# Third stage of a two-layer gated cross-attention model: the causal mask of the fifth unit written by VectorE and ScalarE

## The chip, the cores and the metric

The kernel runs on one core of a Trainium2 chip. The metric is the device time of one execution in microseconds; three executions of the kernel before gave 1333.63, 1334.13 and 1334.41.

## The reference

The model has two layers of gated cross-attention and a gated feed-forward part each, on x of 16 sequences of 128 tokens and 512 channels. The change touches the attention of the second layer only:

```
qp = q @ Wq.T;  k, v = split(latent_kv @ Wkv_expand.T)      # 16 heads of 32
scores = einsum('bhqd,bhkd->bhqk', qh, kh) / sqrt(32)
scores = where(causal, scores, finfo.min)                   # causal, 128 x 128
attn = softmax(scores);  out = (attn @ vh) @ Wout.T
x = x + tanh(g_xattn[1]) * out                              # q is layernorm(x)
```

## The kernel before, in words

The kernel is written by hand for the five engines, each with its own program (`tensor`, `vector`, `scalar`, `gpsimd`, `sync`), and semaphores between them. The order of the work on each engine is the order in which these programs issue it. There is no planner. Four stages follow each other: attention and feed-forward of the first layer, attention of the second (the third stage), feed-forward of the second.

The third stage goes over 16 units, numbered 0 to 15. Unit u stands for a group of four sequences (u // 4) and a group of four heads (u % 4). Its scores fill four banks of PSUM, banks 4 to 7, one for each head j; in a bank each sequence has a block of 128 columns. Per unit:

- TensorE (`scores3`, line 954) writes the mask into each bank: a product of the identity `idb` with the mask `mkb` (bf16, 0 or -1e30) that overwrites the bank. Then 16 products of queries and keys, four per bank, are added to it (`start` is False). Each of them shows as two in the trace.
- VectorE (`largest`, 1920) reads each bank and takes the negated row maxima.
- ScalarE (`exp3`, 1401) reads each bank in four pieces: the exponential with the maximum as bias, and the sum of each row.
- VectorE (`inverse`) inverts the sums, GpSimd multiplies, VectorE's block transposes and a trip through DRAM turn heads 0 and 1, TensorE (`turn3`) turns heads 2 and 3, and TensorE (`av3`) multiplies with the values. ScalarE and VectorE split that result into a rounded part and a remainder (the shape 128x512 into `AR`).

In some units the mask comes another way. `seeded(u)` (line 543) tells them. There `scores3` leaves out the four products, and `seed3(u, j)` copies `mkb` into the bank once the exponentials of unit u - 1 have read it; the banks j in `by_vector(u)` (line 550: bank 0 alone where u % 4 is 1, else 0 and 1) are written by VectorE (line 1915), the others by ScalarE (line 1413). In these units the bank counts as free for TensorE only when `seed3` is done; in the others it is free when the exponentials are. Before the change the units 7, 8, 9, 11, 12, 13 and 15 are seeded.

The programs walk through steps; in step u, TensorE issues: scores of unit u - 1, queries of u (12 products), keys of u (3), values' products of u - 3, the output projection if one is due (from step 7 on), transposes of u - 2, transposes of the next layer norm. VectorE issues in step u: the four maxima of unit u - 1, block transposes of u - 2, the copy of the queries of u, two inverses of u - 1, then `seed3(u, j)` if u is seeded, the copy of the keys of u, the remainder of the values' product, and small work on the layer norm. ScalarE: the exponentials of unit u - 1, the rounding of the values' product of u - 3, `seed3(u, j)` if u is seeded, the copies of the transposed probabilities. In the steps 3 to 7 (`k_first`, line 547) the rounding comes behind all 16 exponentials, and in later steps among them. The scores of unit u itself are issued at the head of step u + 1.

Of the kernel before, what the change touches and what calls it, by code (L numbers as in the profile page):

```python
# [180 lines left out]
def build(nc, i, out):  # L181
    ctx = ExitStack()
    with ctx:
# [357 lines left out]


        def seeded(u):
            return 7 <= u < 16 and u % 4 != 2


        def k_first(u):
# [10 lines left out]
        def exps_over(u, j):  # L558
            return ex_ok["3", u, j] if seeded(u + 1) else ps.drained(("s3", u, j))
# [8 lines left out]
        def tensor(pe):  # L568
# [385 lines left out]
            def scores3(u):  # L954

                ks = [ps.take(("s3", u, j), 4 + j) for j in range(4)]
                pe.wait_ge(*d_ib[1])
                for j in range(4):
                    pe.wait_ge(*ps.free(("s3", u, j)))
                    if not seeded(u):  # L960
                        pe.matmul(blocks3(ks[j]), idb[:, :], mask3, True, False)
                pe.wait_ge(*ps.drained(("q3", u)))
                pe.wait_ge(*ps.drained(("k3", u)))
                for b in range(4):
                    s = slice(128 * b, 128 * b + 128)
                    for j in range(4):
                        ins = pe.matmul(ks[j][:, s], Q3[32 * j:32 * j + 32, s], K3[32 * j:32 * j + 32, s], False, True)
                        if b == 3:
                            ins.then_inc(*ps.fill(("s3", u, j)))
# [166 lines left out]
        def scalar(ac):  # L1136
# [264 lines left out]
            def exp3(u, js):  # L1401
                for j in js:
                    S, k = sm3[:, u % 2, j, :], ps.ap(("s3", u, j))
                    ac.wait_ge(*nb_ok["3", u, j])
                    if u >= 2:
                        ac.wait_ge(*(p3y_ok[u - 2, j] if j < 2 else ps.full(("pt3", u - 2, j))))
                    for b in range(4):
                        c = 512 * j + 128 * b
                        ins = ac.act(P3[:, u % 2, c:c + 128], k[:, 128 * b:128 * b + 128], ACT.Exp, bias=S[:, b:b + 1],
                                     scale=1.0, accum_out=S[:, 4 + b:5 + b])  # L1410
                    ins.then_inc(*(ex_ok.mark(("3", u, j)) if seeded(u + 1) else ps.drain(("s3", u, j), on_act)))
# [1319 lines left out]
```

## Time and profile before

| | |
|---|---|
| median of three runs | 1334.13 us (1333.63 to 1334.41) |
| profiled execution | 1333.26 us |
| its span, first to last instruction | 1331.5 us |
| TensorE busy | 1310.9 us, 98% |
| VectorE busy | 938.0 us, 70% |
| ScalarE busy | 518.0 us, 39% |
| GpSimd busy | 404.9 us, 30% |
| granted TensorE clock, mean | 1.00 |

Times in the rows are microseconds from the start of the span. A line number is that of the helper that issues the operation: L118 a product, L121 a transpose on TensorE, L124 any activation of ScalarE, L127 a copy, L146 the maxima, L130 an operation on two tensors. Tensors that share memory go by one name: `MSK` holds the queries and keys of the third stage, `P` its probabilities, `sm` maxima and sums, `PTV` the turned probabilities. DVE is VectorE, ACT is ScalarE, PE is TensorE.

### The profile page before, as it was taken

To read this page: it belongs to the slowest core of one execution; us is meant where nothing else is said; L and a number is where in the kernel's file an instruction comes from. 1 tells how busy PE (TensorE), PEld (TensorE's weight loads), DVE (VectorE), ACT (ScalarE), POOL (GpSimd) and SP (SyncE) were. 2 spreads that over 40 slices of the span, in tenths; PEclk is the share of its full clock that TensorE was granted. 3 is DMA by queue.
4 is the path that set the end of the run, shared out by engine and by line. 5 is a ranking of instruction groups with operands and counts; after the bars stand their busy time and mean duration, and the time that the engine had idled before them with its cause. 6 is when DMAs were issued, how large, how long until landed. Compare 5 with 4: busy or idle time off the path is not lost.

```text
span 1331.5 us, 20246 instructions
## 1 busy us (share of the span) xinstructions
PE 1310.9 (98%) x7348; PEld 1063.1 (80%) x7348; DVE 938.0 (70%) x1813; ACT 518.0 (39%) x1569; POOL 404.9 (30%) x462
## 2 busy tenths in 40 slices
PE   7999999999999999999999999999998999999998
PEld 6888888888887788878887888788886777778887
DVE  5766676675775878785678668776888888846643
ACT  3545455454564322231113111321127788832220
POOL 4212323231255342201111111113435866630000
PEclk9999999999999999999999999999999999999999
DMA  8755454443572222210121112112334556465651
GB/s 302 236 169 164 148 170 140 154 158 122 187 218 88 86 86 79 80 44 17 52 83 35 50 40 88 44 49 62 93 96 144 191 191 207 159 206 174 215 165 56
DMA packets 135987, 167.92 MB, mean 126 GB/s; under 512 B 16080, under 2 KB 87888, under 8 KB 135888
## 3 DMA queue, kind: packets, MB, share of 16 engines
q1 hardware_dynamic: 135888, 166.63, 39.4%
q8 instruction: 58, 0.95, 0.3%
q14 instruction: 41, 0.34, 0.1%
HBM read 112.05 MB, written 54.53 MB: 125 GB/s over the span
## 4 chain that ended last, share of the span: by engine, by line
PE 89%; DVE 5%; ACT 3%; DMA 1%; issue 1%; POOL 0%; SPq 0%; DVEq 0%; ACTq 0%; POOLq 0%
PE bank L118 87%; ACT P L124 2%; PE bank L121 2%; DVE STG L130 1%; DVE AH L130 1%; DVE st L152 1%; DVE XR L140 1%; DVE sm L146 0%; ACT STG L124 0%; DVE AH L127 0%; ACT AR L124 0%; DMA XR<-in_x_dram 0%; DMA STG<-in_WqT_dram 0%; ACT bank L124 0%; DVE AR L130 0%
## 5 line engine op out<-in xcount | busy, mean ns | idle before, releaser
L118 PE MATMUL bank<-XT,AR 128*128 128x512 f32 x1152 | 279.7, 392 | 0.1
L118 PE MATMUL bank<-AR 128*128 128x512 f32 x1056 | 257.7, 395 | 0.5 <-DVE MSK L136 0.4
L118 PEld LDWEIGHTS bank<-XT,AR 128*128 128x128 f32 x1152 | 214.2, 188 | 47.0 <-ACT STG L124 0.5
L124 ACT ACTIVATE STG<-bank,b1c 128x512 f32<-128x512 f32 x128 | 88.4, 690 | 384.6 <-PE bank L118 309.5
L118 PEld LDWEIGHTS bank<-AR 128*128 128x128 f32 x1056 | 194.4, 188 | 48.5 <-issue 3.1
L118 PE MATMUL bank<-AR,CT 128*128 128x512 f32 x768 | 191.3, 392 | 0.0
L118 PE MATMUL bank<-AR,AH 128*128 128x512 f32 x768 | 185.5, 390 | 0.0
L127 DVE CAST AH<-STG 128x512 fp32r<-128x512 f32 x192 | 90.5, 471 | 110.7 <-PE bank L118 99.0
L118 PEld LDWEIGHTS bank<-AR,AH 128*128 128x128 f32 x768 | 143.9, 188 | 30.0 <-DVE AH L130 0.2
L118 PEld LDWEIGHTS bank<-AR,CT 128*128 128x128 f32 x768 | 140.2, 188 | 26.8
L127 POOL CAST BA<-STG 128x256 fp32r<-128x256 f32 x64 | 30.7, 479 | 393.5 <-PE bank L118 240.8
L130 DVE TENSOR_TENSOR AH<-STG,AH 128x512 fp32r<-128x512 f32 x192 | 141.5, 737 | 6.6
L124 ACT ACTIVATE Pb<-bank,sm 128x128 f32<-128x128 f32 x256 | 90.1, 377 | 89.5 <-DVE sm L136 89.4
L130 POOL TENSOR_TENSOR Pb<-Pb,sm 128x512 f32<-128x512 f32 x64 | 66.7, 1045 | 146.5 <-DVE sm L149 143.9
L118 PE MATMUL bank<-TM,BA 128*128 128x512 f32 x384 | 107.4, 391 | 2.1 <-DVE TM L130 1.3
L124 ACT ACTIVATE P<-bank,sm 128x128 f32<-128x128 f32 x256 | 90.2, 394 | 27.0 <-DVE sm L146 27.0
L118 PE MATMUL bank<-AH,BA 128*128 128x512 f32 x384 | 97.4, 389 | 0.0
L130 DVE TENSOR_TENSOR STG<-STG 128x512 f32<-128x512 f32 x128 | 90.3, 705 | 4.2
L130 DVE TENSOR_TENSOR CT<-bank,CT 128x512 fp32r<-128x512 f32 x64 | 44.1, 689 | 65.9 <-ACT CT L124 65.8
L130 POOL TENSOR_TENSOR rstd<-ve,mhalf 128x1 f32<-128x1 f32 x64 | 38.5, 604 | 169.4 <-DVE ve L136 169.3
L118 PEld LDWEIGHTS bank<-TM,BA 128*128 128x128 f32 x384 | 71.5, 188 | 19.8 <-issue 2.5
L130 POOL TENSOR_TENSOR P<-P,sm 128x512 f32<-128x512 f32 x64 | 66.0, 1050 | 67.2 <-DVE sm L149 67.1
(145 smaller groups left out, 1810.5 us busy)
## 6 DMA issues: line engine op xcount, KB each, us to landing
XR<-scr SPq DMA_DIRECT2D x64, 256.0 KB, 2.9
pscr<-PYZ SPq DMA_DIRECT2D x30, 512.0 KB, 2.9
PYZ<-pscr SPq DMA_DIRECT2D x120, 128.0 KB, 2.9
XR<-in_x_dram SPq DMA_DIRECT2D x32, 256.0 KB, 3.9
XR<-lscr SPq DMA_DIRECT2D x128, 64.0 KB, 2.0
scr<-XR SPq DMA_DIRECT2D x32, 256.0 KB, 2.1
pscr<-STG SPq DMA_DIRECT2D x16, 512.0 KB, 2.6
PTV<-pscr SPq DMA_DIRECT2D x64, 128.0 KB, 2.9
```

The costliest lines, as they stand in the source:

```text
L118: return self.e.matmul(o, w, x, start=start, stop=stop, skip_group_check=True) if self.e else Nothing()
L121: return self.e.transpose(o, x, ident) if self.e else Nothing()
L124: return self.e.activation(o, x, func, **kw) if self.e else Nothing()
L127: return self.e.tensor_copy(o, x) if self.e else Nothing()
L130: return self.e.tensor_tensor(out=o, in0=a, in1=b, op=op) if self.e else Nothing()
L140: return self.e.scalar_tensor_tensor(out=o, in0=a, scalar=s, in1=b, op0=op0, op1=op1) if self.e else Nothing()
L152: return self.e.bn_stats(o, x) if self.e else Nothing()
```

## The change

One line: unit 4, the fifth, joins the seeded units.

```
         def seeded(u):
-            return 7 <= u < 16 and u % 4 != 2
+            return 7 <= u < 16 and u % 4 != 2 or u == 4
```

With it, in unit 4, TensorE issues no mask products. VectorE copies the mask into banks 4 and 5, behind the first two inverses of unit 3 and ahead of the copy of the keys of unit 4. ScalarE copies it into banks 6 and 7, behind the exponentials of unit 3 and the rounding of unit 1's values' product, ahead of the copies of unit 2's transposed probabilities. The functions that do this are not changed:

```
        def seed3(u, j):                                   # ScalarE; VectorE's has e.copy
            ac.wait_ge(*d_ib[1])
            ac.wait_ge(*ex_ok["3", u - 1, j])
            ac.act(blocks3(ps.ap(("s3", u - 1, j))), mask3, ACT.Copy).then_inc(*ps.drain(("s3", u - 1, j), on_act))
```

## Rows read from the trace of the kernel before

**Rows 1.** The page: the chain that ended last, shares by engine.
```profile
PE 89%; DVE 5%; ACT 3%; DMA 1%; issue 1%; POOL 0%; SPq 0%; DVEq 0%; ACTq 0%; POOLq 0%
```

**Rows 2.** That chain in order of time, third stage: start, duration, what.
```profile
1033.35 5.71 ACT P L124 x32
1039.06 0.50 ACT AR L124
...
1039.58 0.69 DVE AR L130
...
1041.34 0.67 DVE sm L146
...
1042.03 5.70 ACT P L124 x32
...
1051.70 0.59 DVE sm L146
...
1059.04 1.53 PE bank L121 x12
```

**Rows 3.** Timeline, TensorE, units 3 to 5: start, duration, operation, count, [idle before].
```profile
1037.20 1.09 PE L121 MATMUL bank<-ident,P 128*128 128x128 f32 x8
...
1038.13 0.81 PE L118 MATMUL bank<-mkb,idb 128*128 128x512 bf16 x3
...
1039.11 0.39 PE L118 MATMUL bank<-mkb,idb 128*128 128x512 bf16 x1 [0.17 <-ACT P L124]
...
1039.43 1.17 PE L118 MATMUL bank<-MSK 32*128 32x128 f32 x32
...
1048.11 1.17 PE L118 MATMUL bank<-MSK 32*128 32x128 f32 x32
```

**Rows 4.** Timeline, VectorE and ScalarE between units 3 and 4.
```profile
1036.96 0.66 DVE L127 COPY MSK<-bank 128x512 f32<-128x512 f32 x1
...
1038.85 0.69 ACT L124 ACTIVATE AR<-bank 128x512 fp32r<-128x512 f32 x1
...
1039.33 1.19 ACT L124 ACTIVATE PTV<-bank 128x512 f32<-128x512 f32 x2
...
1039.58 0.69 DVE L130 TENSOR_TENSOR AR<-bank,AR 128x512 fp32r<-128x512 f32 x1 [1.96 <-ACT AR L124]
```

**Rows 5.** Timeline, VectorE and ScalarE ahead of unit 7, which is seeded.
```profile
1066.88 1.26 DVE L127 CAST bank<-mkb 128x512 f32<-128x512 bf16 x2
...
1068.78 0.69 ACT L124 ACTIVATE AR<-bank 128x512 fp32r<-128x512 f32 x1
...
1069.26 1.22 ACT L124 ACTIVATE bank<-mkb 128x512 f32<-128x512 bf16 x2
```

**Rows 6.** The chain, unit 9: from ScalarE's last mask copy to TensorE's scores.
```profile
1093.78 0.14 issue
```

**Rows 7.** Instructions that read `mkb`, ScalarE's: duration ns min/median/max, first and last start.
```profile
L124 ACT ACTIVATE bank<-mkb x16: 643/649/702, 1069.3 to 1158.6; 128x512 f32<-128x512 bf16 x16
```

**Rows 8.** Timeline, unit 3: scores on TensorE, maxima on VectorE.
```profile
1031.43 1.17 PE L118 MATMUL bank<-MSK 32*128 32x128 f32 x32
...
1032.62 2.48 DVE L146 TENSOR_REDUCE sm<-bank 128x4 f32<-128x512 f32 x4 [0.37 <-PE bank L118]
```

**Rows 9.** TensorE's longest hole of the stage; then windows at the end: busy, clock, DMA.
```profile
1018.34 1.38 PE L121 MATMUL bank<-ident,XR 128*128 128x128 f32 x8 [1.64 <-DVE MSK L136]
...
1330.00:1331.00 1.00, 0.00 (x0) 0.00 (x0) 0.00 (x0) 0.00 (x0) 0.00 (x0) 1.00 0.50 186
1331.00:1331.50 0.50, 0.00 (x0) 0.00 (x0) 0.00 (x0) 0.00 (x0) 0.00 (x0) 0.58 0.00 0
```

**Rows 10.** Timeline, TensorE: its first work, and eight transposes early and late.
```profile
7.04 1.09 PE L121 MATMUL bank<-ident,XR 128*128 128x128 f32 x4 [7.04 <-DVE XR L137]
...
11.77 1.90 PE L121 MATMUL bank<-ident,XR 128*128 128x128 f32 x8
...
1103.43 1.04 PE L121 MATMUL bank<-ident,XR 128*128 128x128 f32 x8
```

## The prediction

> **What bounds the kernel now.** I read the shares of the chain that ended last first: TensorE holds 89% of it [rows 1], so what counts is whether TensorE is ahead or behind where the change falls. Then the same chain piece by piece in the third stage [rows 2]. Up to 1059.04 us it is not on TensorE there. It runs: the 16 exponentials of unit 3 on ScalarE (5.71 us from 1033.35), the rounding of the values of unit 1 (0.50), its remainder on VectorE (1039.58), some small VectorE work, the first maximum of unit 4 (1041.34), the exponentials of unit 4 (1042.03). At 1059.04 it goes over to TensorE and stays there but for a few pieces. So the fifth unit lies in the one part of the stage where TensorE is not the bound, and TensorE's work there is worth its time only where a piece of that chain waits for it.
>
> Third, the timeline of TensorE between units 3 and 4 [rows 3]. It ends its eight transposes at 1037.20 + 1.09 = 1038.29. The first three mask products stand beside their end, the fourth starts at 1039.11, just behind the exponentials (1033.35 + 5.71 = 1039.06), because it rewrites the last bank that they read. The scores of unit 4 follow at 1039.43. The products therefore fill a time in which the scores could not start anyway: only 1039.43 - 1039.06 = 0.37 us lies between the last exponential and the scores.
>
> **What is removed.** Four products: 0.81 us for three and 0.39 for one [rows 3], 1.20 us busy on TensorE. As a saving it is worth at most the 0.37 us just named, and that only if nothing is put in its place. I book nothing for it by itself, since the new start of the scores is worked out below from what they now wait for. If the cover were gone (if TensorE were the bound here) it would be worth up to 1.20 us. The Trainium skill, page "TensorE: Matmul & The Clock Gate", section on the 56 ns gap, gives 215.7 ns from start to start for a product of 512 columns at the full clock; by it the four would be worth an estimated 0.86 us.
>
> **What is added on VectorE.** Two copies of the mask into banks 4 and 5, between the inverses and the copy of the keys of unit 4. In unit 7, the first that is served this way, two such copies take 1.26 us [rows 5]. The bank they need is free: the inverses ahead of them wait for the same exponentials. The key copy then starts at 1036.96 + 1.26 = 1038.22 in place of 1036.96 [rows 4] and ends at about 1038.9, still ahead of the scores. VectorE was idle for 1.96 us ahead of 1039.58, waiting for ScalarE's rounding [rows 4]; 1.26 fits in. Cost 0. Without that idle time it would be 1.26 us on the chain.
>
> **What is added on ScalarE.** Two copies into banks 6 and 7, queued behind the last exponential and behind the rounding of the values of unit 1 (the branch `k_first`). I take the place from unit 7, which has the same order: rounding at 1068.78, the two copies from 1069.26 to 1069.26 + 1.22 = 1070.48, that is 1.70 us behind the rounding's start [rows 5]. In unit 4 the rounding starts at 1038.85 [rows 4], so the copies end at 1040.55. Behind them are queued the two evacuations of transposed probabilities, 1039.33 before [rows 4], now about 1040.4 to 1041.6. ScalarE then waits for the first maximum of unit 4 anyway, so these delay nothing. The rounding itself stays ahead of the copies, so VectorE's piece of the chain at 1039.58 stays where it is.
>
> **The new wait.** The scores of unit 4 now wait for the last ScalarE copy. In unit 9, where TensorE already stands for such a copy, the gap from its end to the scores is 0.14 us [rows 6]. So they start at 1040.55 + 0.14 = 1040.69 in place of 1039.43: 1.26 us later. Bounds: the longest such copy in the trace took 702 ns [rows 7], and two of them end to end behind the rounding's own 0.50 us [rows 2] and with a 0.14 gap give 1038.85 + 0.50 + 1.40 + 0.14 = 1040.89, plus some 0.2 if the rounding has to finish its whole record: 1.66 us late. From below, two copies that overlap as well as the two evacuations at 1039.33 (1.19 us) [rows 4] give 1.23. I take 1.26, since unit 7 has the very order.
>
> **How much of it reaches the chain.** Where the maxima wait for the scores, the first starts 1.19 us behind the scores' start (1031.43 to 1032.62) [rows 8]. Before, the scores of unit 4 were ready for it at 1039.43 + 1.19 = 1040.62, while VectorE came to it only at 1041.34 [rows 2]: 0.72 us of slack. Now they are ready at 1040.69 + 1.19 = 1041.88. The first maximum, and with it the exponentials of unit 4, come 1041.88 - 1041.34 = **0.54 us later**. With the bounds of the wait: 0.51 to 0.94.
>
> **What is late next.** On TensorE, 1040.69 plus the whole 8.68 us between the scores of units 4 and 5 (1039.43 to 1048.11) [rows 3] is 1049.37 at the latest, and 1.19 more is 1050.56. The first maximum of unit 5 was at 1051.7 on the chain [rows 2], which hangs on the exponentials of unit 4 and so moves to 1052.2: that unit's scores are not missed. From there to 1059.04 the chain is VectorE's and ScalarE's work at one piece after another, and it moves as a whole. Behind 1059.04 TensorE works with hardly a gap, so nothing gives the 0.54 us back. No DMA issue is added, and none is moved past another; the transfer of unit 2's probabilities that TensorE's value products wait for starts from an earlier VectorE transpose, and so arrives as before.
>
> **Sum.** Profiled execution: 1333.26 us (span 1331.5 and 1.76 around it), + 0.54 = 1333.80. The median of the runs shown is 0.87 above it, 1334.13; I forecast 1334.13 + 0.54 = **1334.7 us**. A measurement of this kernel tells a change from none at about 0.2%, 2.7 us; this is far inside.
>
> **The rivals.**
> A, the removed products come off in full: TensorE's time is what counts, and the copies are covered. For it: 89% of the chain is TensorE's [rows 1], and from unit 7 on the scores start with no wait. Against it: in this part the chain is not TensorE's [rows 2]. It gives 1334.13 - 1.20 = 1332.9. By the page's figure above it would be an estimated 1333.3.
> B, no cover at the maximum: the late scores pass on in full, because VectorE's small work moves too, or because a waiting maximum starts later than in unit 3. 1334.13 + 1.26 to 1.66 = 1335.4 to 1335.8. Against it: the slack of 0.72 us comes from VectorE pieces that hang on the rounding, which is ahead of the copies.
> C, all covered: the copies overlap better and the remaining wait is swallowed before 1059.04: 1334.1. Against it: no piece of the chain after 1041.34 shows a free wait.
> D, slower beyond the limit: TensorE's clock falls in the new hole. TensorE is idle from 1038.29 to 1040.69, 2.40 us, longer than the longest hole of this stage, 1.64 us ahead of 1018.34 [rows 9]. It decides if the granted clock goes from the upper level (2.4 GHz) to the lower (1.2 GHz) before 1040.69. The price from this trace: TensorE's first work, after 7.04 us of standing still, ran slow: eight transposes took 1.90 us at 11.77, against 1.04 for the same eight at 1103.43 [rows 10]. The slow stretch lasts from 7.04 to about 13.67, 6.6 us, and at that ratio 6.6 x (1 - 1.04/1.90) = 3.0 us are lost. Time: 1334.13 + 0.54 + 3.0 = 1337.7. Against it: TensorE stops at about 1328.1, the clock still reads 1.00 in 1330:1331 and is lower only in the last half microsecond, 0.58 [rows 9]. So it held for some 2.9 us of idleness there, and for 1.64 us here. The Trainium skill says on the same page, section "The HAM clock gate", that an idle TensorE falls back to the lower clock and that the moment isn't tied to the kernel's own work. By that rule the hole is not safe merely for being shorter than one that held; the row still makes the fall unlikely.
>
> **Chances.** Forecast (0.4 to 1.0 us later) 60%; B 15%; C 12%; A 8%; D 4%; anything else 1%. The range reaches from A's side to B with the 0.4 us by which the runs shown lie around their median (1333.63 to 1334.41): 1333.0 to 1336.2. It leaves out D and part of A. A, B, C and the forecast all lie within 0.2%. So slower by more than 0.2% is D and a little, 4%; faster by more would need more than twice the removed work, 2%; within 0.2% 94%.
>
> **What would show it.** After the change: 32 mask products, 14 copies of the mask on VectorE and 18 on ScalarE; between units 3 and 4 TensorE stands idle for about 2.4 us, ended by a ScalarE copy; the scores of unit 4 start some 3.5 us behind the start of the transposes ahead of them; the first maximum of unit 4 idle before it for about 0.5 us and ended by TensorE; the exponentials of unit 4 starting 9.2 us behind those of unit 3 in place of 8.68; the granted clock at 1.00. Each unit from 7 on should keep its length. I am wrong if the exponentials of units 3 and 4 stand 8.7 us apart or less (A or C), if they stand 9.9 or more apart (B), or if products after the hole take longer than before it (D). If the interval is as I say but the end of the kernel is not later, something between 1042 and 1059 had slack that the chain did not show.

## The result and the profile after

| | before | after |
|---|---|---|
| median of 22 executions each | 1334.81 us (1333.63 to 1336.53) | 1336.88 us (1335.31 to 1338.58) |
| ratio | | 1.0013, 95% interval 1.0007 to 1.0019 |
| profiled execution | 1333.26 us | 1335.31 us |
| its span | 1331.5 us | 1333.2 us |
| outside the span | 1.76 us | 2.11 us |

Executions that jumped to 1628 us or more, which came up in the kernel before too, are left out of all medians, counts and ratios below.

The change makes the kernel slower by 0.13% by the ratio, about 1.7 us (0.9 to 2.5); the two medians lie 2.07 us apart. I had forecast 0.54, and the time lies above the range of 1333.0 to 1336.2. Of the 2.18 us between 1336.88 and the forecast of 1334.7, 0.68 us is the kernel before itself: its median was 1334.13 in the three runs shown and 1334.81 in the 22.

The page: span, then busy time, share and number of instructions of each engine. Four products fewer on TensorE, two copies more on VectorE and two on ScalarE (1569 before).

```profile
span 1333.2 us, 20244 instructions
...
PE 1311.2 (98%) x7344; PEld 1064.2 (80%) x7344; DVE 939.8 (70%) x1815; ACT 519.9 (39%) x1571; POOL 405.4 (30%) x462
```

The timeline of the changed kernel between units 3 and 4, all engines (start, duration, operation, count, [idle before and what ended it]); it answers to [rows 3 to 5].

```profile
1037.05 1.26 DVE L127 CAST bank<-mkb 128x512 f32<-128x512 bf16 x2
...
1037.28 1.10 PE L121 MATMUL bank<-ident,P 128*128 128x128 f32 x8
...
1038.97 0.68 ACT L124 ACTIVATE AR<-bank 128x512 fp32r<-128x512 f32 x1
...
1039.45 1.21 ACT L124 ACTIVATE bank<-mkb 128x512 f32<-128x512 bf16 x2
1039.69 0.69 DVE L130 TENSOR_TENSOR AR<-bank,AR 128x512 fp32r<-128x512 f32 x1 [0.78 <-ACT AR L124]
...
1040.92 2.05 PE L118 MATMUL bank<-MSK 32*128 32x128 f32 x32 [2.55 <-ACT bank L124]
...
1042.90 4.42 PE L118 MATMUL bank<-AR 128*128 128x512 f32 x15
1042.91 2.48 DVE L146 TENSOR_REDUCE sm<-bank 128x4 f32<-128x512 f32 x4 [1.37 <-PE bank L118]
```

Up to the scores all is as foreseen: VectorE's copies fit into its idle time (1.96 has become 0.78), the rounding and its remainder keep their place, ScalarE's copies end 1.69 us behind the rounding's start, and TensorE stands idle for 2.55 us until a ScalarE copy ends. Then the scores take 2.05 us in place of 1.17, and the 15 products behind them 4.42 in place of about 3.7. The windows of the same trace say why. The last three numbers of a line are the granted clock, the DMA share and GB/s.

```profile
1038.40:1040.90 2.50, 0.00 (x0) 0.01 (x1) 1.72 (x4) 2.50 (x9) 1.37 (x3) 1.00 0.29 88
1040.90:1041.90 1.00, 0.98 (x19) 1.00 (x22) 0.56 (x4) 0.77 (x2) 0.97 (x2) 0.56 0.83 238
1041.90:1042.90 1.00, 1.00 (x22) 0.78 (x17) 0.00 (x0) 0.00 (x0) 1.00 (x2) 0.50 0.94 201
...
1043.90:1044.90 1.00, 1.00 (x5) 0.79 (x4) 1.00 (x3) 1.00 (x7) 1.00 (x1) 0.74 0.94 342
1044.90:1045.90 1.00, 1.00 (x6) 0.82 (x5) 1.00 (x2) 1.00 (x7) 0.46 (x1) 1.00 0.16 59
```

Through the whole gap the clock reads 1.00. At 1041.0, when the scores have just begun, it goes to 0.50 (from 2.4 to 1.2 GHz), and at 1044.4 it comes back. It is the prediction's rival D, but later than D's condition had it (a fall before 1040.69). The Trainium skill ("TensorE: Matmul & The Clock Gate", section "The HAM clock gate") states that an idle TensorE falls back to half its clock; the trace agrees in the level, 0.50 behind a gap of 2.55 us, and shows the fall only once TensorE had resumed.

The chain that ended last, in order of time (start, duration, what), of the changed kernel; it answers to [rows 2].

```profile
1033.45 4.37 ACT P L124 x25
...
1039.65 1.02 ACT bank L124 x2
1040.67 0.24 issue
1040.92 1.97 PE bank L118 x29
1042.88 0.02 issue
1042.91 0.70 DVE sm L146
1043.61 0.02 issue
1043.63 5.72 ACT P L124 x32
...
1053.93 4.32 ACT P L124 x24
```

The chain no longer takes VectorE's small work; it goes through ScalarE's copies and TensorE's slow scores. I use one mark from here on: the time from the first exponential of unit 3 to the first of unit 4. It was 1042.03 - 1033.35 = 8.68 [rows 2] and is 1043.63 - 1033.45 = 10.18. The next such distance, unit 4 to unit 5, is 10.30; in the kernel before it was 10.28, from 1042.03 to this piece of the same chain:

```profile
1052.31 4.30 ACT P L124 x24
```

So the profiled difference of 2.05 us (1335.31 - 1333.26) is made up of 0.10 ahead of unit 3, 1.50 in the mark, 0.02 in the next unit, 0.08 behind it, and 0.35 outside the span.

### The profile page after: what moved, and what is told of

Same layout as the page of the kernel before. It is cut to its first block, busy times and chain, and to the rows that moved or that the text cites. A ratio compares the mean times of both kernels' runs of the same rounds, so it can differ in the third digit from the quotient of the medians.

```text
span 1333.2 us, 20244 instructions
## 1 busy us (share of the span) xinstructions
PE 1311.2 (98%) x7344; PEld 1064.2 (80%) x7344; DVE 939.8 (70%) x1815; ACT 519.9 (39%) x1571; POOL 405.4 (30%) x462
## 4 chain that ended last, share of the span: by engine, by line
PE 88%; DVE 6%; ACT 4%; DMA 1%; issue 1%; POOL 0%; SPq 0%; ACTq 0%; DVEq 0%; POOLq 0%
PE bank L118 87%; ACT P L124 2%; PE bank L121 2%; DVE STG L130 1%; DVE AH L130 1%; DVE XR L140 1%; DVE AH L127 0%; ACT STG L124 0%; DVE st L152 0%; DVE sm L146 0%; ACT bank L124 0%; ACT AR L124 0%; DMA XR<-in_x_dram 0%; DMA STG<-in_WqT_dram 0%; DVE TM L130 0%
```

## The experiments

Two theories at first. CLOCK: the mark grows by the 0.54 of the prediction, and by more where the clock falls. WAIT: all of the 1.50 is waiting, or scores onto copied banks are slow. Each expectation was written before its run. What was measured is collected in one table behind them.

**The gap filled.** TensorE multiplies into a bank that is free; the edit stands ahead of `scores3(u - 1)` in TensorE's program:

```
                if u == 5:
                    spare = ring3.banks[ring3.n % 4]
                    pe.wait_ge(*ps.drained(ps.last[spare]))
                    for _ in range(8):
                        pe.matmul(blocks3(ps.banks[spare]), idb[:, :], mask3, True, True)
```

> The changed kernel, and in the gap ahead of the scores of unit 4 TensorE multiplies eight times identity by mask into the spare bank that the queries of unit 5 overwrite next (work without use, about 1.7 us). The mark is the time from the first exponential of unit 3 to the first of unit 4: 8.68 us before the change, 10.18 after it. Theory CLOCK (the gap of 2.5 us lets the granted clock fall to 0.50, which makes the scores slow): the gap shrinks to under 1 us, the clock stays at 1.00, the scores take 1.17 and not 2.05, the mark is 9.2 to 9.3, and the time is before + 0.6, about 1 us under the changed kernel. Theory WAIT (everything lost is the wait for the mask copies, or scores onto copied banks are slow): mark 10.2 as without the filling.

**With three products in place of eight** (`range(3)`).

> As the filled kernel, with three products without use in place of eight (about 0.8 us): the gap of 2.5 us is cut into about 0.6 and 1.0 us. CLOCK: the clock stays at 1.00 in most executions, mark 9.2 to 9.3, time as the kernel with eight, before + 0.6 to 1. If the share of work in the stretch counts and not the longest gap, the clock may still fall: mark up to 10.2.

**Late scores, no seeding.** In `scores3`, behind the mask products:

```
+                if u == 4:
+                    pe.wait_ge(*ps.drained(("pt3", 2, 3)))
                 for b in range(4):
                     ...
```

> The kernel before, all mask products kept; the scores of unit 4 wait in addition, behind the products, until ScalarE has evacuated the transposed probabilities of unit 2 (about 1040.6). Scores as late as in the changed kernel, but the gap ahead of them only some 1.2 us. CLOCK: the clock stays at 1.00, scores 1.17 us long, mark 9.2 to 9.3 (the 0.54 of the prediction), time before + 0.5 to 0.6. WAIT (late scores alone explain the loss): mark 10.0 to 10.2 and time before + 1.5 to 2.

**The gap ahead of the products, no seeding.** The same wait, ahead of them:

> The kernel before, no mask copied by another engine in unit 4; the same additional wait, but ahead of the mask products of unit 4, so that TensorE has a gap of about 2.3 us and then the products and scores. CLOCK: the gap alone makes the clock fall; products 0.4 us apart in place of 0.21, scores 2.05, mark 11.5 to 12, time before + 3 to 4. WAIT: clock 1.00, products and scores at their usual length, mark 10.1, time before + 1.4.

**Either half of the change.** `seeded` gets the bank as a second argument: `or u == 4 and j < 2`, and `or u == 4 and j >= 2`.

> Of the change only VectorE's part: in unit 4 banks 4 and 5 get the mask by a copy of VectorE, banks 6 and 7 by a product as before. CLOCK: TensorE has no gap over 1 us, and VectorE's copies lie in its idle time: mark 8.6 to 8.8, clock 1.00, time as before within 0.3 us. WAIT in the form that VectorE's copies or the copied banks cost: mark 9.2 or more.

> Of the change only ScalarE's part: in unit 4 banks 6 and 7 get the mask by a copy of ScalarE, banks 4 and 5 by a product. The products of banks 4 and 5 stand behind the transposes, then TensorE waits for ScalarE some 2.1 us. CLOCK: a gap of over 2 us still lets the clock fall in most executions, scores 1.2 to 2.05 us long by where it falls, mark (first exponential of unit 3 to first of unit 4) 9.2 with the clock kept and up to 10.2 without it, time before + 1 to 2. WAIT: mark 9.2 to 9.3 and no more. In either case it shows whether ScalarE's copies bring the 0.35 us that the changed kernel takes more outside its span (2.1 against 1.76): yes if it is 2.1 here.

**The changed kernel again, twice.**

> The changed kernel once more, beside the others on their chip, for a second profile. CLOCK: the fall comes at this gap again, the mean clock reads 0.999 or less in all executions, mark between 9.8 and 10.2 by where in the scores the fall comes, time before + 1.5 to 2.1. If the fall of the first profile was chance, the mark is 9.2 here.

> The changed kernel a third time, for where the fall of the clock comes. The two profiles so far had it 0.1 us behind the start of the scores (mark 10.18) and behind their end (mark 9.34). CLOCK: it falls again behind the gap, somewhere between the gap's end and two or so us later, the mark between 9.2 and 10.2; mean clock below 1.000 in all executions.

**ScalarE's copies ahead of the rounding.** In ScalarE's program `seed3(4, j)` for j of 2 and 3 is moved ahead of `av3(u - 3)`.

> The changed kernel with ScalarE's two copies ahead of the rounding of unit 1's values and not behind it. The scores can then start about 0.5 us earlier (gap 2.05 us), but the rounding comes 1.0 us later, and with it VectorE's remainder and small work, which stand ahead of the first maximum. By the chain as the prediction reads it: first maximum at 1041.34 + 1.03, mark 9.7 if the clock is kept, and 9.7 to 10 where it falls in the scores, since VectorE's work is then what is late. If ScalarE's copies were all that delays (WAIT without VectorE's chain), the mark would be under 9.2.

**What is outside the span.** First: unit 4 as in the change, `and not (u == 8 and j >= 2)` added for unit 8. Second: the kernel before, with each ScalarE mask copy of unit 7 issued as two of 256 columns.

> The changed kernel, and in unit 8 banks 6 and 7 get their mask by a product again, so that ScalarE executes as many instructions as before the change (1569 in place of 1571) while unit 4 is served as in the change. The changed kernel takes 2.11 us outside its span, the one before 1.76. If it is the number of ScalarE's instructions: 1.76 to 1.85 here. If it is what happens in unit 4: 2.1. The mark (first exponential of unit 3 to first of unit 4) stays 9.3 to 10.2 with the clock lower for 3.4 us behind the gap (CLOCK).

> The kernel before, unit 4 untouched; in unit 7 ScalarE's two copies of the mask are cut into two instructions of half the width each, so that it executes 1571 instructions as in the changed kernel. If their number brings the 0.35 us outside the span: 2.1. If it is what happens in unit 4: 1.76 to 1.85. The mark is 8.68 in either case.

**Another place for VectorE's copies.** `or u in (10, 14) and j < 2`.

> The kernel before, and in units 10 and 14, where TensorE is the bound and all four products are still issued, VectorE copies the mask into banks 4 and 5; banks 6 and 7 keep their product. Two products of 0.21 us less in each: if TensorE is the bound there, the scores of each come 0.4 us earlier and the time is before - 0.8. If VectorE's 1.26 us in each makes the copy of the keys or the values' remainder late, it is 0 or up to + 1.

What they gave. "Gap" is TensorE's idle time ahead of the scores (in the fourth row ahead of the products, in the filled kernels ahead of the filling, with three products behind it too). "Clock falls at" is the start of the 0.1 us window in which the clock leaves 1.00, in the profiled execution. "Low" counts the executions whose mean clock reads below 1.000; it doesn't say where in the kernel the clock fell. The ratio is to the kernel before on the same chip.

| kernel | gap, us | mark, us | clock falls at | outside span | low | ratio (95% interval) |
|---|---|---|---|---|---|---|
| before | 0.17 | 8.68 | not | 1.76 | 16 of 100 | 1 |
| change | 2.55 | 10.18 | 1041.0 | 2.11 | 22 of 22 | 1.0013 (1.0007 to 1.0019) |
| late scores | 1.16 | 9.18 | not | 1.85 | 3 of 11 | 1.0009 (1.0000 to 1.0018) |
| gap, then products | 2.30 | 10.94 | 1043.2 | 1.78 | 9 of 11 | 1.0018 (1.0009 to 1.0026) |
| filled, 8 | 0.59 | 9.26 | not | 2.18 | 2 of 11 | 1.0011 (1.0002 to 1.0020) |
| filled, 3 | 0.57, 1.01 | 9.24 | not | 2.13 | 5 of 11 | 1.0012 (1.0003 to 1.0021) |
| VectorE's half | 0.40 | 8.67 | 1030.0 | 1.74 | 1 of 11 | 1.0000 (0.9991 to 1.0009) |
| ScalarE's half | 1.95 | 10.06 | 1041.2 | 2.13 | 8 of 9 | 1.0015 (1.0006 to 1.0025) |
| change, again | 2.54 | 9.34 | 1043.4 | 2.11 | 11 of 11 | 1.0013 (1.0004 to 1.0022) |
| change, third | 2.50 | 9.33 | 1042.2 | 2.11 | 10 of 10 | 1.0010 (1.0001 to 1.0019) |
| copies first | 2.04 | 9.72 | 1042.7 | 2.18 | 8 of 10 | 1.0011 (1.0002 to 1.0020) |
| change, unit 8 half by product | 2.55 | 9.36 | 1043.2 | 1.79 | 8 of 8 | 1.0008 (0.9998 to 1.0018) |
| before, copies of unit 7 cut | 0.18 | 8.66 | not | 2.14 | 1 of 8 | 1.0002 (0.9992 to 1.0012) |
| VectorE's half in 10 and 14 | 0.20 | 8.68 | not | 1.80 | 2 of 11 | 1.0012 (1.0002 to 1.0021) |

The ratios tell the kernels apart badly: executions of the kernel before lie up to 5.8 us apart (1332.81 to 1338.62), and in these profiles the work ahead of unit 3 alone ends between 1033.35 and 1035.76. The mark doesn't have that noise. So what follows is shown for the mark; that the filled kernels are faster than the changed one by the clock's share, as expected, the times don't show (1.0011 and 1.0012 against 1.0010 to 1.0013).

**The clock, shown.** With the gap filled the copied banks are still copied and the scores nearly as late, and they take 1.17 us again. TensorE and ScalarE in the timeline of that kernel:

```profile
1035.18 0.37 ACT L124 ACTIVATE P<-bank,sm 128x128 f32<-128x128 f32 x1 [1.68 <-DVE sm L146]
...
1040.69 1.90 PE L118 MATMUL bank<-mkb,idb 128*128 128x512 bf16 x8 [0.59 <-DVE MSK L127]
1042.52 1.17 PE L118 MATMUL bank<-MSK 32*128 32x128 f32 x32
1043.63 3.70 PE L118 MATMUL bank<-AR 128*128 128x512 f32 x15
...
1044.44 0.37 ACT L124 ACTIVATE P<-bank,sm 128x128 f32<-128x128 f32 x1 [1.06 <-DVE sm L146]
```

1044.44 - 1035.18 = 9.26. Of the 0.92 between this and 10.18, 0.1 is an earlier start of the scores (7.34 us behind the first exponential of unit 3, against 7.47), and the rest is the slow clock. The other way round, a gap alone brings the fall with no bank copied. The kernel with the gap ahead of the products, and two of its windows:

```profile
1042.12 1.04 PE L118 MATMUL bank<-mkb,idb 128*128 128x512 bf16 x4 [2.30 <-ACT PTV L124]
1043.09 2.03 PE L118 MATMUL bank<-MSK 32*128 32x128 f32 x32
1045.06 4.43 PE L118 MATMUL bank<-AR 128*128 128x512 f32 x15
```

```profile
1043.10:1043.20 0.10, 0.10 (x5) 0.10 (x5) 0.00 (x0) 0.00 (x0) 0.10 (x1) 1.00 0.93 213
1043.20:1043.30 0.10, 0.10 (x4) 0.10 (x8) 0.00 (x0) 0.00 (x0) 0.10 (x1) 0.53 0.66 195
```

The four products behind the gap still run at full speed (1.04), and the scores behind them do not. I had expected slow products too, and a mark of 11.5 to 12; it is 10.94. The fall comes 1.1 us after TensorE is back at work. WAIT has fallen with these two. What they don't separate is the length of the gap from what TensorE did ahead of it: in every profile with a fall behind the new gap its eight transposes stand there (in ScalarE's half two products behind them).

**The wait, shown.** The kernel with late scores has their delay without the long gap:

```profile
1033.93 0.37 ACT L124 ACTIVATE P<-bank,sm 128x128 f32<-128x128 f32 x1 [1.68 <-DVE sm L146]
...
1041.22 1.17 PE L118 MATMUL bank<-MSK 32*128 32x128 f32 x32 [1.16 <-ACT PTV L124]
...
1043.11 0.37 ACT L124 ACTIVATE P<-bank,sm 128x128 f32<-128x128 f32 x1 [2.03 <-DVE sm L146]
```

Its mark, 9.18, is 0.50 over 8.68. And with ScalarE's copies first, where by the same reading of the chain VectorE's remainder is late and not the scores, the mark was 9.72; 9.7 with the clock kept, up to 10 without it, was expected.

**Where the fall comes decides its price.** The changed kernel again, TensorE and VectorE:

```profile
1041.98 1.17 PE L118 MATMUL bank<-MSK 32*128 32x128 f32 x32 [2.54 <-ACT bank L124]
1043.09 5.29 PE L118 MATMUL bank<-AR 128*128 128x512 f32 x15
...
1043.14 2.48 DVE L146 TENSOR_REDUCE sm<-bank 128x4 f32<-128x512 f32 x4 [0.55 <-PE bank L118]
```

And a window of its low stretch (the clock is the third number from the end):

```profile
1043.40:1046.80 3.40, 3.40 (x10) 2.60 (x9) 3.40 (x6) 2.93 (x17) 2.92 (x3) 0.51 0.69 235
```

The stretch at 0.50 lasted 3.4 us in all seven profiles of these kernels that have a fall behind the new gap. TensorE loses 1.6 us by it each time: here 5.29 - 3.70, in the first profile 2.05 - 1.17 and 4.42 - 3.70. But here the scores were done before it, VectorE waited 0.55 us for them as forecast (0.54), and the products of unit 5 had slack. The mark is 9.34, and the clock adds nothing to it: the 0.1 over the filled kernels is the later start of the scores. In the first profile the stretch began in the scores, which are on the chain, and added 10.18 - 9.34 = 0.84. I had expected 9.8 to 10.2 here, with the clock low in every execution: the low readings came, 11 of 11, the mark did not, because the fall came behind the scores and not in them.

**Each half.** VectorE's copies cost nothing: mark 8.67, ratio 1.0000. ScalarE's alone bring a gap of 1.95 us, the fall, the 0.35 us outside the span and nearly the whole mark, 10.06. In VectorE's half the clock falls too, though the gap ahead of its scores is 0.40 us; the fall, at 1030.0, lies behind gaps that the kernel before has as well (0.44 us, then 1.43):

```profile
1029.88 0.95 PE L121 MATMUL bank<-ident,XR 128*128 128x128 f32 x4 [1.43 <-POOL XR L137]
```

```profile
1029.50:1030.00 0.50, 0.12 (x1) 0.15 (x2) 0.00 (x0) 0.50 (x3) 0.50 (x2) 1.00 0.06 25
1030.00:1030.50 0.50, 0.50 (x4) 0.50 (x4) 0.22 (x1) 0.50 (x2) 0.41 (x2) 0.54 0.02 8
```

That is also where the 16 of 100 may come from; the one profile of the kernel before has no fall there. Those 16 have a median of 1336.0 us, the other 84 one of 1334.25.

**Outside the span.** The pages of the two kernels, first the change with unit 8 half by product, then the kernel before with the copies of unit 7 cut:

```profile
PE 1312.0 (98%) x7346; PEld 1064.8 (80%) x7346; DVE 938.9 (70%) x1815; ACT 517.2 (39%) x1569; POOL 404.9 (30%) x462
```

```profile
PE 1311.1 (98%) x7348; PEld 1063.1 (80%) x7348; DVE 937.0 (70%) x1813; ACT 517.3 (39%) x1571; POOL 404.6 (30%) x462
```

1569 instructions on ScalarE and 1.79 us outside the span with the change in; 1571 and 2.14 us without it. All 14 profiles fall into the two groups: 1569 and 1.74 to 1.85, or 1571 and 2.11 to 2.18. So do all the other executions whose span is on record: 1.74 to 1.87, or 2.06 to 2.19. The 0.35 us go with the length of ScalarE's program and not with what happens in unit 4.

**Units 10 and 14.** Expected 0.8 us less, or 0 to 1 more if the copies make the keys or the remainder late; measured 1.2 us more (from the first exponential of unit 5 to the end 280.37 against 279.19). VectorE and TensorE in unit 10:

```profile
1102.21 1.26 DVE L127 CAST bank<-mkb 128x512 f32<-128x512 bf16 x2
1103.38 0.68 DVE L130 TENSOR_TENSOR AR<-bank,AR 128x512 fp32r<-128x512 f32 x1
...
1104.11 1.66 PE L118 MATMUL bank<-AR 128*128 128x512 f32 x6 [0.87 <-DVE AR L130]
```

The copies stand ahead of the values' remainder, which holds a bank that TensorE needs next: 0.87 us of waiting for two products saved, and 0.86 the same way in unit 14. So it was the second case, a little beyond its bound. No kernel tried beats the one before.

## Why the prediction was wrong

- **The chain** was read rightly: TensorE not the bound here, the removed products worth nothing, VectorE's copies free, no slack up to 1059.04. The distance between units 4 and 5 stayed (10.28 and 10.30), and the rest of the kernel too (279.19 and 279.27).
- **The new wait** was right within 0.13 us. Scores 1.26 us late was forecast; from the first exponential of unit 3 to the scores it is 7.47 (1040.92 - 1033.45) against 6.08 before, so 1.39 late. The time from the end of ScalarE's copy to TensorE is 0.24 and not 0.14. In the filled kernels the distance to the scores is 7.34 and 7.35.
- **The first maximum 0.54 late** was right without the clock: marks of 9.18, 9.24 and 9.26, and 9.33 to 9.36 where the fall comes late, against the 9.22 forecast.
- **Rival D is the step that failed, in its chance.** I gave it 4% and forecast a clock of 1.00. It came in all four profiles with this unit 4, and the mean clock reads below 1.000 in 43 of 43 executions of the change. The reason I gave against it was that at the kernel's end the clock still read 1.00 some 2.9 us after TensorE's last product [rows 9]. But the fall isn't seen during the gap. In the changed kernel it came 0.1 to 1.4 us after TensorE had resumed, so a clock that reads 1.00 a while into an idle time doesn't show that a gap of that length does no harm. The 1.64 us gap of [rows 9] was no bound either: the clock held behind it in that execution, and in VectorE's half it fell behind gaps of 0.44 and 1.43 us.
- **Its price was too high**: 3.0 us from the start of the kernel [rows 10]. TensorE lost 1.6, and the chain nothing or 0.84, by where the fall came. Nor does the trace show that the slow start was a low clock: the transposes of 11.77 took 1.90 us while the clock column reads 1.00.

```profile
10.00:12.00 2.00, 2.00 (x12) 2.00 (x12) 2.00 (x3) 0.16 (x1) 2.00 (x3) 1.00 0.99 389
```

- **Two signs of being wrong** came with it: products behind the gap took longer (D), and the first profile's mark, 10.18, was over 9.9. That second sign was meant for rival B, yet the 0.72 us of slack ahead of the maximum was there; it was the clock that pushed the mark up.
- **A term was missing**: 0.35 us outside the span, from two more instructions on ScalarE. I had taken what lies around the span as fixed.
- **The range** took its bottom and top from three runs. The median of the kernel before was 0.68 us higher in the 22 that go with the result, and 0.2 to 0.4 higher in the later 100 (1334.31 to 1334.52 by chip).

From before, 1334.81: 0.54 + 0.1 for the later start + 0.35 + 0 to 0.84 for the clock give 1335.8 to 1336.6, that is 1.0 to 1.8 over before; the measured interval is 0.9 to 2.5. The two later rounds of the change fit it, 1335.83 over 1334.52 and 1335.30 over 1334.31; the 2.07 between the first medians is 0.2 more than it explains. Without a costly fall the sum stays inside the range (1335.8); with one, but from the median that I had, it does too (1334.7 + 0.1 + 0.35 + 0.84 = 1336.0). It took the clock and the higher median together to leave it. What decides where behind a gap the fall comes, and what share of the executions has the costly place, stays open: three profiles show one such and two others. Whether three products in the gap protect worse than eight (5 low of 11 against 2) is within chance; but 5 of 11 is more than the 16 of 100 of the kernel before, so that three are enough is not shown. Why two ScalarE instructions cost 0.35 us is not explained.

## What to carry to other kernels

Moving work off TensorE where TensorE isn't the bound of a stretch earned nothing here and opened a gap; before doing it, ask what TensorE does in the freed time and whether the clock holds through it. Look for the clock after a gap, not in it, and at the matmuls behind it. When a difference is under a few microseconds, compare one distance inside the trace that the change alone can move, and split off what lies outside the span, which can change as well.

## What was not expected of the hardware

The clock fell up to 1.6 us after TensorE had resumed (copies first: scores at 1041.11, fall at 1042.7). In all seven profiles with a fall behind the new gap it stayed at 0.50 for 3.4 us although TensorE was busy throughout. In the six kernels run later with a gap of 1.95 to 2.55 us the mean clock read below 1.000 in 54 of 59 executions. In the profiles of the changed unit 4 TensorE started 0.24 to 0.28 us after the copy that released it, against 0.14 in unit 9, where it had been idle for 0.19 us only. The length of the idle time alone doesn't explain it: in ScalarE's half it started 0.09 us after the copy, with 1.95 us idle before. Why is open.
